# A six-layer network inside a four-layer kernel: feed-forward of four tiles at once, values by transfers, scaling on POOL, a new order of every engine

## The reference, cut to what matters

```python
for i in range(DEPTH):                       # 6
    x = attn_layer(shift_tokens(x), Wqkv[i], q_scale[i], k_scale[i], Wo[i]) + x
    x = ffn_layer(shift_tokens(x), ln_g[i], ln_b[i], W1[i], b1[i], W2[i], b2[i]) + x
# attn_layer: q, k, v of 16 heads of 64; q and k get l2norm, a scale and a rotary turn;
#   local attention: windows of 32, each query sees 32 keys back; softmax(8 q k) v; then Wo
# ffn_layer: layer norm; hg = xn @ W1 + b1 (128 -> 2*341); a, gate = halves
#   a * gelu(gate) @ W2 + b2
# shift_tokens: the second half of the features comes from the token before
```

## Time and profile before

| what | value |
|---|---|
| median of three runs | 5718.36 us |
| profiled execution | 5696.51 us |
| its span in the profile | 5694.7 us |
| mean granted clock of PE | 0.889 of 2.4 GHz |
| busy PE / DVE / ACT / POOL | 78 / 63 / 52 / 34% of the span |
| instructions | 89214 |

### The profile page before, as it was taken

The page is one execution under the profiler, slowest core; times in us unless marked ns, Lnnn a source line. Parts: engine busy times, 40 slices in busy tenths (PEclk is TensorE's granted clock), DMA queues, the critical chain, the costliest instruction groups (busy, mean ns, idle before and its releaser), DMA issues. The chain is left out here.

```text
span 5694.7 us, 89214 instructions
## 1 busy us (share of the span) xinstructions
PE 4468.9 (78%) x28284; PEld 3096.7 (54%) x28284; DVE 3603.6 (63%) x7261; ACT 2963.1 (52%) x8154; POOL 1958.8 (34%) x1203
## 2 busy tenths in 40 slices
PE   6887987888644458888888888888888888588788
PEld 4655665555411136666666666666666666355566
DVE  5554224455578867777777777777777777344422
ACT  3333434443233336666666666666666666233433
POOL 3433003232045444444444444444444434122300
PEclk8888999999755579999999999999999999566799
DMA  0000000000000010000000000000000000000000
GB/s 18 1 2 35 0 0 20 1 1 14 3 0 0 0 50 1 0 0 22 0 0 22 0 0 22 0 0 22 0 0 0 0 0 1 17 1 0 0 30 7
DMA packets 26280, 41.43 MB, mean 7 GB/s; under 512 B 12112, under 2 KB 18664, under 8 KB 25448
## 3 DMA queue, kind: packets, MB, share of 16 engines
q1 hardware_dynamic: 26088, 39.04, 2.0%
HBM read 36.93 MB, written 2.10 MB: 7 GB/s over the span
## 5 line engine op out<-in xcount | busy, mean ns | idle before, releaser
L1426 PE MATMUL ps<-l2f_wqkv,l2f_xsT 128*128 (+3 forms) x1536 | 741.4, 605 | 97.1 <-DVE xnT L1621 90.3
L1358 POOL TENSOR_TENSOR l2f_rn<-l2f_ss,neghalf 128x16 f32<-128x16 f32 x192 | 564.7, 2941 | 436.1 <-DVE l2f_ss L1615 436.1
L1803 ACT ACTIVATE l2f_p<-ps,l2f_negmax 128x96 f32<-128x96 f32 x1536 | 501.7, 338 | 282.7 <-DVE l2f_negmax L1646 279.1
L1364 POOL TENSOR_TENSOR l2f_cosd<-xnT,l2f_rot 128x1024 f32<-128x1024 f32 x192 | 487.2, 2542 | 174.8 <-DVE xnT L1621 174.8
L1484 PE MATMUL ps<-l2f_pT,l2f_vw 96*128 96x128 f32 x3072 | 423.1, 281 | 40.4 <-DVE l2f_pT L1668 40.4
L1426 PEld LDWEIGHTS ps<-l2f_wqkv,l2f_xsT 128*128 128x128 f32 (+1 forms) x1536 | 243.4, 178 | 347.8 <-issue 197.4
L1818 ACT COPY l2f_oT<-ps 64x256 f32<-64x256 f32 x768 | 281.3, 366 | 269.8 <-PE ps L1484 258.3
L1484 PEld LDWEIGHTS ps<-l2f_pT,l2f_vw 96*128 96x128 f32 x3072 | 381.7, 195 | 61.4 <-issue 56.5
L1384 POOL TENSOR_TENSOR l2f_rstd<-l2f_mv,neghalf 128x1 f32<-128x1 f32 x96 | 52.8, 550 | 1051.5 <-DVE l2f_mv L1680 1051.5
L1457 PEld LDWEIGHTS ps<-l2f_kT,l2f_qz 128*128 128x128 f32 x3072 | 399.2, 194 | 1.4 <-issue 0.3
L1457 PE MATMUL ps<-l2f_kT,l2f_qz 128*128 128x96 f32 x3072 | 398.7, 273 | 0.0
(11 more groups left out here) (354 smaller groups left out, 10607.0 us busy)
## 6 DMA issues: line engine op xcount, KB each, us to landing
l2f_wqkv<-L_ffn_Wqkv_dram SPq DMA_DIRECT2D x18, 512.0 KB
l0f_w<-L_w_dram SPq DMA_DIRECT2D x2, 2304.0 KB
l3f_w<-L_w_dram SPq DMA_DIRECT2D x2, 2048.0 KB
l2f_wo<-L_ffn_Wo_dram SPq DMA_DIRECT2D x6, 512.0 KB
l2f_w<-L_ffn_W_dram SPq DMA_DIRECT2D x6, 341.0 KB
l2f_b<-L_ffn_b_dram SPq DMA_DIRECT2D x6, 341.0 KB
l1f_w<-L_w_dram SPq DMA_DIRECT2D x1, 1152.0 KB
k_turn<-l3a_kF SPq DMA_DIRECT2D x4, 256.0 KB, 2.0
```

The lines of the kernel that those rows point to most:

```text
L1358: nc.gpsimd.tensor_tensor(rn[:, k], ss[:, k], g.neghalf[:, 0:HEADS], ALU.pow).then_inc(rn_ready, 1)
L1364: nc.gpsimd.tensor_tensor(cosd[:, k].rearrange("p (h d) -> p h d", d=DH), nrm[:, k].rearrange("p (h d) -> p h d", d=DH), rot[:, k, 0, t].u ...
L1426: ins = nc.tensor.matmul(g.ps[0:rows, 2 * (k % 2) + hf], x, wqkv[:, bass.ds(weight_slot(it), 1), c0 + hf * 512:c0 + (hf + 1) * 512] .rearr ...
L1803: ins = nc.scalar.activation(p[:, n % 2, c], g.ps[:, 4, c * KW:(c + 1) * KW], ACT.Exp, bias=negmax[:, col:col + 1], accum_out=rowsum[:, co ...
```

## The change

- The feed-forward runs once an iteration for the four tiles of the iteration before: the normalized tiles are collected in `xnT2` [128, 2, 512], three gate products (`gates`, slot 1) and three half products (`halves`, slot 2) with the weights as the stationary operand give the hidden state already transposed, and `feed` (slot 3) makes 12 products in one bank. ACT's `copy_gates` adds the gate's bias, one `gelu` covers 128x1536, DVE's `gate_hidden` adds the other bias and multiplies in one instruction. The bias rides in six more columns of `w1`; POOL copies the layer's `w1` to `w1c` each iteration (`fix_weights`). `b1` has no tile and no transfer of its own (11 transfers a layer).
- `yb` plus the output projection goes to a new tile `ym`, two iterations deep; `rot` and `lnd` are two deep as well.
- Values: one projection of 128 rows in banks 0, 1, one copy to `vt` (two deep), then two or three transfers from SP to the windows in `vw` (`move_values`); SP's weight loads stand between them in the same queue.
- Scaling: DVE keeps the reciprocal (`inverse_sums`), POOL does the multiplication (`scale`).
- Waits: one counter for q, k and v each where there was one; waits that the old order implied are written out; PE's `read` waits name who has to be through with a bank. `CREDIT`, the start value of the counters, is 16 instead of 4.
- Order: every engine's `slot` is another. `tile(it, t, 2)` is two tiles ahead, `fed` the iteration before. The loop's body holds two iterations, and there are two leading slots and four closing ones.

```diff
-CREDIT = 4
+CREDIT = 16
-    NLOAD = 12
+    NLOAD = 11
+            def move_values(it, t):
+                w = QBS * (t % 2)
+                sp.wait_ge(v_copied, at(it, TILES, t + 1))
+                sp.wait_ge(pv_done, at(it, STEPS2, PER * (t - 1)))
+                if t:
+                    sp.dma_start(vw[0:WINDOW, w], vt[P - WINDOW:P, (t - 1) % 2]).then_inc(v_moved[t % 2], 16)
+                sp.dma_start(vw[WINDOW:KW, w], vt[0:QB, t % 2]).then_inc(v_moved[t % 2], 16)
+                sp.dma_start(vw[:, w + 1], vt[P - KW:P, t % 2]).then_inc(v_moved[t % 2], 16)
+            for it in range(ITERATIONS):
+                for t in range(TILES):
+                    move_values(it, t)
+                if it % BATCH == 0 and it // BATCH + 1 < DEPTH:
+                    load_weights(it // BATCH + 1)
 POOL
-                inverse_deviation(*behind)
-                inverse_norms(*ahead, 0)
-                scaled_rotary(*ahead)
-                inverse_norms(*ahead, 1)
-                cosines(*ahead, 0)
-                cosines(*ahead, 1)
+                scaled_rotary(it, t)
+                cosines(*tile(it, t, 1), 0)
+                fix_weights(it, t)
+                scale(*tile(it, t, 0), 0)
+                inverse_deviation(*tile(it, t, -1))
+                scale(*tile(it, t, 0), 1)
+                inverse_norms(*tile(it, t, 1), 1)
+                scale(*tile(it, t, 0), 2)
+                cosines(*tile(it, t, 1), 1)
+                scale(*tile(it, t, 0), 3)
+                inverse_norms(*tile(it, t, 2), 0)
 PE, slot after the change, its waits left out
+                mix(-1) scores(0, 1) shift(-1) project(1, v) turn(0, 0) scores(0, 2) turn_xn2(-1)
+                gates(0) pv(0, 0) turn(0, 1) halves(0) feed gates(1) turn_qk(1, q) pv(0, 1) gates(2)
+                scores(0, 3) turn_y(2) turn(0, 2) halves(1) project(2, q) turn_qk(1, k) halves(2)
+                pv(0, 2) turn(0, 3) scores(1, 0) pv(0, 3) project(2, k)
 DVE
+                norms(ch, *tile(it, t, 1), 1)
+                inverse_sums(*tile(it, t, 0), 1)
+                normalize_shifted(*tile(it, t, -1))
+                copy_probs(*tile(it, t, 0), 0)
+                maxima(*tile(it, t, 0), 2)
+                rotate(ch, *tile(it, t, 1), 0)
+                copy_probs(*tile(it, t, 0), 1)
+                gate_hidden(*fed(it, t), 0)
+                inverse_sums(*tile(it, t, 0), 2)
+                normalize(*tile(it, t, 1), 1)
+                fetch(*tile(it, t, 2))
+                feed_out(*fed(it, t))
+                swap(ch, *tile(it, t, 1), 1)
+                maxima(*tile(it, t, 0), 3)
+                rotate(ch, *tile(it, t, 1), 1)
+                gate_hidden(*fed(it, t), 1)
+                inverse_sums(*tile(it, t, 0), 3)
+                copy_probs(*tile(it, t, 0), 2)
+                norms(ch, *tile(it, t, 2), 0)
+                copy_probs(*tile(it, t, 0), 3)
+                gate_hidden(*fed(it, t), 2)
+                maxima(*tile(it, t, 1), 0)
+                normalize(*tile(it, t, 2), 0)
+                swap(ch, *tile(it, t, 2), 0)
+                mix_out(*tile(it, t, 0))
+                inverse_sums(*tile(it, t, 1), 0)
+                maxima(*tile(it, t, 1), 1)
+                moments_of(ch, *tile(it, t, 0))
 ACT
+                affine(*tile(it, t, -1))
+                exps(ch, *tile(it, t, 0), 2)
+                copy_gates(*fed(it, t), 0)
+                copy_outputs(*tile(it, t, 0), 0)
+                copy_gates(*fed(it, t), 1)
+                copy_q(*tile(it, t, 1))
+                copy_gates(*fed(it, t), 2)
+                copy_outputs(*tile(it, t, 0), 1)
+                shift_copies(*tile(it, t, 2))
+                exps(ch, *tile(it, t, 0), 3)
+                squares(*tile(it, t, 2), 0)
+                copy_k(*tile(it, t, 1))
+                copy_outputs(*tile(it, t, 0), 2)
+                gelu(*fed(it, t))
+                copy_outputs(*tile(it, t, 0), 3)
+                exps(ch, *tile(it, t, 1), 0)
+                squares(*tile(it, t, 2), 1)
+                exps(ch, *tile(it, t, 1), 1)
+                copy_values(*tile(it, t, 2))
```

More of the change, by code:

```diff
@@ L1549, in slot, with hidden @@
[L1549 to L1575 removed]
+            def hidden(f, c, c0):
+                pe.wait_ge(w1_ready, at(f, 1, 1))
+                pe.wait_ge(xnT2_ready, at(f, TILES, TILES))
+                r0, rows = CH[c]
+                return nc.tensor.matmul(g.ps[0:rows, 7], w1c[:, f.odd, c0 + r0:c0 + r0 + rows], xnT2[:, f.odd],
+                                        start=True, stop=True)
@@ new lines, in gates, with halves, feed @@
+            def gates(f, t, c):
+                if t == 1:
+                    hidden(f, c, DI).then_inc(gates_ready, 1)
+            def halves(f, t, c):
+                if t == 2:
+                    hidden(f, c, 0).then_inc(halves_ready, 1)
+            def feed(f, t):
+                if t != 3:
+                    return
+                pe.wait_ge(hT_ready, at(f, 3, 3))
+                for n in range(TILES):
+                    for c, (r0, rows) in enumerate(CH):
+                        ins = nc.tensor.matmul(g.ps[:, 7, n * P:(n + 1) * P], hg[0:rows, c, n * P:(n + 1) * P],
+                                               w2[0:rows, bass.ds(weight_slot(f), 1), c].rearrange("p a c -> p (a c)"),
+                                               start=(c == 0), stop=(c == 2))
+                ins.then_inc(ff_ready, 1)
@@ L1699, in gate_hidden @@
[L1699 to L1714 removed]
+                rows = CH[c][1]
@@ L1720, in mix_out @@
                 dve.wait_ge(mixed, at(it, TILES, t + 1))
-                nc.vector.tensor_tensor(yb[:, t], yb[:, t], g.ps[:, 6, 0:D], ALU.add).then_inc(y_mixed, 1)
-            def slot(ahead, now, behind):
-                fetch(*ahead)
-                mix_out(*behind)
-                maxima(*now, 0)
-                affine_of(*behind)
-                moments_of(ch, *behind)
-                scale(*now, 0)
-                normalize_shifted(*behind)
-                maxima(*now, 1)
-                norms(ch, *ahead, 0)
-                copy_probs(*now, 0)
-                scale(*now, 1)
-                maxima(*now, 2)
-                norms(ch, *ahead, 1)
-                copy_probs(*now, 1)
-                normalize(*ahead, 0)
-                scale(*now, 2)
-                maxima(*now, 3)
-                bias_hidden(*behind, 1)
-                swap(ch, *ahead, 0)
-                normalize(*ahead, 1)
-                scale(*now, 3)
-                copy_probs(*now, 2)
-                bias_hidden(*behind, 0)
-                rotate(ch, *ahead, 0)
-                gate_hidden(*behind)
-                swap(ch, *ahead, 1)
-                copy_probs(*now, 3)
-                rotate(ch, *ahead, 1)
-                feed_out(*behind)
@@ L1839, in slot @@
[L1839 to L1857 removed]
+                    nc.scalar.activation(xnT2[:, it.odd, t * P:(t + 1) * P], g.ps[:, 7, 0:P], ACT.Identity,
+                                         bias=lnd[:, it.odd, 1:2], scale=lnd[:, it.odd, 0:1]).then_inc(xnT2_ready, 1)
@@ new lines, in copy_gates, with gelu @@
+            def copy_gates(f, t, c):
+                if t != 1:
+                    return
+                rows = CH[c][1]
+                act.wait_ge(gates_ready, at(f, 3, 1 + c))
+                act.wait_ge(ff_ready, at(f, 1, 0))
+                nc.scalar.activation(hg[0:rows, c], g.ps[0:rows, 7], ACT.Identity,
+                                     bias=w1c[0:rows, f.odd, HB + 3 + c:HB + 4 + c]).then_inc(hg_ready, 1)
+            def gelu(f, t):
+                if t != 1:
+                    return
+                act.wait_ge(hg_ready, at(f, 3, 3))
+                nc.scalar.activation(hg[:], hg[:], ACT.Gelu).then_inc(gelu_ready, 1)
```

580 lines of the change are left out of this document (364 added, 216 removed).

## The result

The changed kernel takes 5474.87 us (median of 4 runs, 5458.1 to 5495.8) against 5727.75 for the kernel before, run beside it (5703.35 to 5739.79): ratio 0.9565, interval 0.9516 to 0.9614. It is 4.4% faster; I had said 9.3%, with a range that ended at 5370. The profiled execution took 5480.16 us, its span is 5478.4.

What follows compares the result with a forecast made beforehand. Bound: a chain passing between engines in hand-written order, PE's work as floor. 96 slots x (29.06 - 23.35) = 548, less 16 for the ends, takes 532 from 5696.5: 5165, or 5190 on the median's scale; range 5050 to 5370.

Steps and rivals of the forecast that it cites:

- The loop's jump: Each iteration: loop's branch, scaled rotary and weights copy lie where POOL waits; together 0.7 us, bounds 0 to 5.
- The swap: DVE's pair of swap multiplications, contending with POOL's cosines for memory: 2.5 us, bounds 1.25 to 3.6.
- the ring: Chain over DVE, POOL and ACT that closes last in a slot, two swaps in it: 22.0 us.
- The feed-forward slots: Feed-forward of the iteration before lengthens slot 1 by 2.3, slot 2 by 1.45, slot 3 by 0.95 us.
- PE's floor: PE's work in one slot after the change: 22.2 us as recorded, 21 where blocks follow without a gap.
- POOL's scaling: Four 128x384 scalings a slot move from DVE to POOL: 0.83 us each, +3.3; bounds of one 0.56 and 1.2.
- transfers: SP's value transfers take 6 us, with 23 available, so hidden; weights queued before them also 0, bounds 0 and 10 a layer.
- The ends: Stage's start and end: +13 us behind the last mix (26 to 28 against 14.6), +3 for two leading slots.
- B: Rival: DVE-POOL lock costs its upper bound and POOL delays the probabilities; 25.6 us a slot, 5400 us; chance 0.20.
- A: Rival: POOL rarely gets ahead of DVE, so PE becomes the bound; 21.9 us a slot, 5047 us; chance 0.15.
- C: Rival: value transfers gate the slot, 31.0 us at 30 us of landing; slower, 5920 us; chance 0.03.
- D: Rival: interlocks of the new order hold the slot at 29 us, no change, 5720 us; chance 0.02.

Runs made afterwards that it cites:

- e1: Changed kernel without its loop, all 24 iterations of the stage written one after the other: 5389.7 us, ratio 0.9450 to the kernel before.
- e2: Changed kernel with a loop body of four iterations instead of two: 5422.3 us, ratio 0.9526 to the kernel before.
- e3: Kernel before the change with a loop body of two iterations instead of one: 5769.1 us, ratio 1.0146 to the kernel before.
- e9: Changed kernel with a loop body of one iteration, POOL's cosines waiting for both swap halves, and first weights loaded earlier: 5362.0 us, ratio 0.9386.
- e4: Changed kernel with POOL's cosines of k waiting until both halves of DVE's swap are done: 5376.7 us, ratio 0.9460 to the kernel before.
- e8: Changed kernel with TensorE's feed-forward cut (hidden products of 16 columns, output product for one tile of four): 5341.2 us, ratio 0.9376.
- e10: Changed kernel with POOL's cosines waiting for both swap halves and TensorE's feed-forward work cut to almost nothing: 5294.2 us, ratio 0.9275.
- e6: Changed kernel without the transfers of values and the waits for them, the buffer staying zero: 5439.1 us, ratio 0.9530 to the kernel before.
- e7: Changed kernel with the scaling of the probabilities put back from POOL on DVE: 5589.5 us, ratio 0.9798 to the kernel before.
- e5: Changed kernel without its loop, POOL's cosines after both swap halves, first weights loaded before the wait for constants: 5304.5 us, ratio 0.9307.

## Why the prediction was wrong, step by step

The stage gained 263 us where I had 532. The 269 that are missing, from the distances: ordinary iterations 100.3 - 93.4 = 6.9, times 24, 166; nine jumps at 9.2, 83; the remaining 20 are the first slots and the two ends. Two steps of the prediction failed: the price of the loop's jump, which was put at next to nothing without a reason that covers it, and the swap under the lock at 2.5 us.

- **The loop's jump.** "Scaled rotary, the weights copy on POOL and the loop's branch ... bounds 0 to 5, I take 0.7." This term is mis-sized by 9.2 / 2 = 4.6 us an iteration, and its reason ("where POOL waits anyway") doesn't cover it: the stop is on PE and DVE, not on POOL. In the kernel before a jump costs 1.1 us at most by the distances (116.7 against 115.6), and I took the loop to be as cheap after the change, without asking whether the body, twice as long, still stays loaded. e1, e2, e3 and e9 show it: 83 us.
- **The swap.** "I take 2.5, which is the middle and the contended row." It is 3.45, next to the upper bound of 3.6. The row at 2.52 was one in which POOL had begun before both halves; with both released by the same `normalize` the case in the order of the code is the upper one: first half, POOL, second half. I had worked out that sequence as the bound and then taken the middle. The Trainium skill (SBUF — State Buffer, section "Who interferes with whom") says that who issues first holds the shared path for the whole instruction; the 3.45 of two halves and 2.86 of the cosines agree, with the lock changing hands between DVE's two instructions. In the prediction's own sum the measured 3.45 makes the ring 22.0 + 2 x 0.95 = 23.9 a slot and the iteration 4 x 23.9 + 5.4 = 101.0, and 100.3 are measured: this one term, corrected, covers all of the 6.9. Taken out of the kernel it gives back less, 3.2 us an iteration (e4), 77 of the 166, because the slots then stop at the limit below it, 22.10 in slot 0. The two readings overlap, so the 166 can't be divided between the swap and the next step in one way only.
- **The feed-forward slots.** "+2.3", "+1.45", "+0.95". In the changed kernel these held: from mix to mix slots 1, 2 and 3 are 1.8, 1.0 and 0.4 us above the shorter slot 0 of 24.12. They would have failed had the lock cost nothing: in e4 they are about 3.0, 2.3 and 3.0 above 22.10, 8.3 where I had 4.7, so "slack takes the most" is true only behind the lock. With e4's 97.1 the iteration is still 3.7 above my 93.4; e8 and e10 give TensorE's work 1.5 to 2.0 of it. What sets the rest wasn't taken apart; the round trips through ScalarE and VectorE are a guess.
- **The plain ring.** With the swap's measured price the walk gives 23.9, and slot 0 of the changed kernel is 24.12 in the shorter of its two kinds (25.4 in the other): the walk of the four orders was nearly right once its price is. The 22.10 of e4 against my 22.0 is luck, since the same ring has 19.6 there.
- **PE's floor, POOL's scaling, table loads, transfers.** 22.2 forecast and 22.0 measured; 0.83 and 0.826; as forecast; 0 and, by e6, not distinguishable from 0. The Trainium skill's price for the scaling (GPSIMD Engine Reference, section 3.1), cited in the prediction, would have been 1.1; this case has 0.826, and the mean of the 384 scalings on DVE in e7 is 0.675, some of them held up to 2.42.
- **The ends.** I had 16 us for both, 13 behind the last mix and 3 in front. From the start of the last mix to the last output it is 32.6 us, where I had 26 to 28 and the kernel before 14.6: 18.0 more. The lead is 2 us longer in front of the first transpose and 7.5 from there to the first mix: the first projection waits for the weights until 2061.34, since SyncE waited for `band_ready` before it issued them. e5 took the 7.5 back.
- **The rivals.** B, the lock at its upper bound, is the nearest: 25.6 a slot against 25.1 in the ordinary iterations, 5400 and, with 83 us of jumps, 5483. Its second half, that POOL passes its delays to the turns of the probabilities, is hardly in the trace: from 2107 to 4522 PE waited 7.8 us in all for POOL's scalings and its weight loads 26.8. I gave B 0.20 and let the range end at 5370, below its own price. It had no jump in it either, so that it comes so near to 5475 with them is partly luck. A and C fell (PE 86% busy in the stage; e6), and D too.

## What to carry to other kernels

Before a loop's body is made longer, look at the instruction transfers and at one jump in the trace: a body of one iteration is repeated here almost without instruction transfers, one of two is fetched anew in every pass, and that can take back a good part of what a change saves (83 us beside the 263 of this one). Where two engines are released by the same instruction and share a path to memory, price the case that the code's order makes, here the upper bound, and not the mean of the bounds. And when a contended operation is freed, expect only what the next limit leaves: 12.7 us of VectorE's time an iteration came back as 3.2. When a number comes out as forecast, check that its terms did too: e4's 22.10 against my 22.0 came from another limit than the one I had added up.

## What the runs showed of the hardware that I had not expected

The same work in the same order is 73 us slower when the loop's body holds two iterations instead of one (e3), with instruction transfers of 5.6 MB instead of 2.4. An iteration with such a jump is 4.9 to 10.5 us longer than the others in the eight kernels that have them, about the same for a body of two (9.2) as for one of four (9.3, e2). The limit lies, for these kernels, between one iteration and two; which engine's stream exceeds it wasn't tested. The Trainium skill (Trainium Architecture — The Big Picture, section "The software stack") says that the instruction streams are moved into each engine's instruction memory when the program is loaded; here instructions are still transferred in the middle of the execution, from 2300 to 4300 one packet in the kernel before and 209 in e3, and their amount depends on the loop, so the measurement decides. The stop comes with the burst of transfers at the jump and not with transfers as such: e1 has 183 packets from 2300 to 4300 and no stop of PE longer than 0.2 us that the profile calls "issue". Straight code isn't free either: 0.9 to 1.3 us an iteration (e5 against e4, e1 against the changed kernel), for which no cause was found.
